# Two attentions on one core: projections of the self attention spread over twice as many blocks, and the weighted sum cut in two by queries

## The reference, cut to what matters

```python
qkv = x @ w_qkv.T                                  # self attention
scores = einsum('bhqd,bhkd->bhqk', q, k) * scale + bias
out = einsum('bhqk,bhkd->bhqd', softmax(scores), v)
x = layernorm(x + out @ w_proj.T + b_proj)         # called x1 in the kernel
scores = einsum('bqhd,bkhd->bhqk', x, ctx) * scale2
x = layernorm(x + einsum('bhqk,bkhd->bqhd', softmax(scores), ctx))   # x2
x = layernorm(x + experts(x))                      # not touched by the change
```

## Time and profile before

| what | value |
|---|---|
| three timed runs | 1044.22, 1048.89 and 1048.36 us; median 1048.36 us |
| profiled execution | span 1045.2 us from the first to the last instruction; no other time of its own is given |
| busy in that span | PE 934.1 us (89%), ACT 747.5 us (72%), DVE 703.3 us (67%), POOL 297.5 us (28%) |
| the 16 bodies | from 37.3 us to about 716 us of the span; the expert stage follows |

### The profile page before, as it was taken

One profiled execution on the slowest core, in us unless ns is written; L12 is line 12 of the kernel. 1 busy time (PEld: TensorE's weight loads), 2 busy tenths in 40 slices (PEclk: granted clock), 3 DMA queues, 4 the chain that ended last, 5 costly groups with the idle time before them and its releaser, 6 DMA issues. The chain is left out here.

```text
span 1045.2 us, 17700 instructions
## 1 busy us (share of the span) xinstructions
PE 934.1 (89%) x5301; PEld 514.6 (49%) x5301; DVE 703.3 (67%) x1836; ACT 747.5 (72%) x1414; POOL 297.5 (28%) x337
## 2 busy tenths in 40 slices
PE   5599999999999999999999998996189999999991
PEld 2133444444444433333333333332179988988991
DVE  5277777677787788356556565585457887887883
ACT  1378777787878778899898895893047766766761
POOL 4043132231404111011222123123323534444443
PEclk9699999999999999999999997997589999999996
DMA  7989596978687675987876793751263533443450
GB/s 208 207 229 251 109 256 143 316 142 252 143 247 187 185 201 88 181 199 161 160 155 114 157 174 68 144 120 41 76 216 115 202 137 121 169 180 127 163 208 30
DMA packets 74844, 172.04 MB, mean 165 GB/s; under 512 B 16657, under 2 KB 36039, under 8 KB 64712
## 3 DMA queue, kind: packets, MB, share of 16 engines
q1 hardware_dynamic: 67944, 156.36, 60.4%
q0 software_dynamic: 6496, 14.16, 3.9%
q10 hardware_dynamic: 320, 0.52, 0.1%
HBM read 122.23 MB, written 53.73 MB: 168 GB/s over the span
## 5 line engine op out<-in xcount | busy, mean ns | idle before, releaser
L742 ACT ACTIVATE probs<-sc 128x512 f32<-128x512 f32 x1024 | 528.9, 608 | 117.7 <-DVE sc L829 80.4
L497 PE MATMUL sc<-qst,kst 57*128 57x512 f32 (+1 forms) x1024 | 268.4, 473 | 18.2 <-DMA qst<-s_qk 12.8
L829 DVE TENSOR_TENSOR sc<-sc,strip 128x308 f32<-128x308 f32 (+1 forms) x512 | 192.8, 430 | 101.2 <-PE sc L497 100.5
L509 PE MATMUL ot<-probs,vals 128*32 128x512 f32 x1600 | 214.0, 607 | 0.1
L497 PEld LDWEIGHTS sc<-qst,kst 57*128 57x128 f32 (+1 forms) x1024 | 118.6, 187 | 191.8 <-ACT probs L742 147.7
L1691 ACT ACTIVATE f_h<-f_h_ps,par 128x384 f32<-128x384 f32 x104 | 60.9, 586 | 31.0 <-PE f_h_ps L1601 31.0
L1768 DVE TENSOR_TENSOR f_h_lo<-f_h,f_h_hi 128x384 fp32r<-128x384 f32 x104 | 73.4, 706 | 13.7 <-DVE f_h_hi L1766 5.7
L1849 POOL DMA_INDIRECT home<-s_x,get_ids x45 | 53.6, 1190 | 72.5 <-issue 42.4
L1766 DVE CAST f_h_hi<-f_h 128x384 fp32r<-128x384 f32 x104 | 37.1, 356 | 39.7 <-ACT f_h L1691 39.5
L509 PE MATMUL ms<-probs,vals 128*32 128x512 f32 x448 | 61.9, 627 | 0.0
L1862 POOL DMA_INDIRECT out<-f_normed,f_put_ids x39 | 43.1, 1106 | 64.6 <-ACT f_normed L1725 56.1
(11 more groups left out here) (189 smaller groups left out, 1604.7 us busy)
## 6 DMA issues: line engine op xcount, KB each, us to landing
s_qk<-w_hi SPq DMA_DIRECT2D x32, 512.0 KB, 7.3
strip<-in_w_all SPq DMA_DIRECT2D x16, 1024.0 KB, 7.7
f_raw<-in_w_all SPq DMA_DIRECT2D x14, 1024.0 KB, 6.3
s_x<-x SPq DMA_DIRECT2D x8, 1026.0 KB, 11.0
kst<-s_qk SPq DMA_DIRECT2D x32, 256.0 KB, 6.1
qst<-s_qk SPq DMA_DIRECT2D x32, 256.0 KB, 7.2
s_x_parts<-split SPq DMA_DIRECT2D x16, 512.0 KB, 8.8
kst<-s_ctx_parts SPq DMA_DIRECT2D x32, 256.0 KB, 6.6
```

What stands on the lines that cost most here:

```text
L497: nc.tensor.matmul(sc[j][:], kst[at:at + rows, i, P * c:P * c + P], qst[at:at + rows, i, :], start=True, stop=True).then_inc(scored, 1)
L509: last = nc.tensor.matmul(sums_bank(n, g)[32 * j:32 * j + 32, :], vals[:, c, 4 * g + j, :], probs[:, k % KEPT, j, :], start=(c == 0), stop ...
L742: nc.scalar.activation(probs[:, k % KEPT, j, :], sc[j][:], ACT.Exp, scale=scale).then_inc(exped, 1)
L829: nc.vector.tensor_tensor(sc[j][:, lo:hi], sc[j][:, lo:hi], band_backwards(rank_of(4 * g + j), at, hi - lo), ALU.add).then_inc(biased, 1)
```

## The change

It does four things. `attend` takes the place of `scores` and `weigh_behind`: in each block of both attentions PE now makes two heads' scores, the weighted sum of 256 queries, the other two heads' scores, and the weighted sum of the other 256 queries. `project_qk` is cut in two by input channels (d = 0 and 1, three matmuls each): queries and keys of pair 0 are made in blocks 0 to 3, those of pair 1 in blocks 12 to 15. The output projection and the values begin one block earlier. The tiles of PSUM are assigned anew, so that one transpose of x1 moves from block 15 to block 1 of the next body, and its store a body later. The x of batch b+2 gets a buffer of its own (`later_xT`, in the space of `x2`), is loaded before the store of x1, and POOL splits it in two halves.

```diff
-            def scores(n, k):
+            def scores(n, k, two):
...
-                for j in range(4):
+                for j in range(2 * two, 2 * two + 2):
...
-                pe.wait_ge(exped, UNITS * n + 4 * k + 4)
+                if half == 0:
+                    pe.wait_ge(exped, UNITS * n + 4 * k + 4)
                 for j in range(4):
-                    last = nc.tensor.matmul(sums_bank(n, g)[32 * j:32 * j + 32, :], vals[:, c, 4 * g + j, :],
-                                            probs[:, k % KEPT, j, :], start=(c == 0), stop=(c == NC - 1))
-                last.then_inc(summed, 1)
...
+                    last = nc.tensor.matmul(sums_bank(n, g)[32 * j:32 * j + 32, some], vals[:, c, 4 * g + j, :],
+                                            probs[:, k % KEPT, j, some],
+                                            start=(c == 0 and half == 0), stop=(c == NC - 1 and half == 1))
+                if half == 1:
+                    last.then_inc(summed, 1)
...
+            def attend(n, k):
+
+                for half in range(2):
+                    scores(n, k, half)
+                    weigh_behind(n, k, half)
...
-            def project_qk(b, i):
...
+            def project_qk(b, i, d):
...
+                terms = [term for term in terms_of(b) if term[2] == d]
...
-                if 5 <= k < 9:
-                    project_out(b, k - 5)
-                if k in (14, 15):
-                    turn_x1(b, 15 - k)
+                if k == 1 and b > 0:
+                    turn_x1(b - 1, 0)
+                if 4 <= k < 8:
+                    project_out(b, k - 4)
+                if k == 14:
+                    turn_x1(b, 1)
+                if k == 15 and b == B - 1:
+                    turn_x1(b, 0)
...
                 if k < 4:
-                    project_qk(b, k)
-                if 9 <= k < 13:
-                    project_v(b, (k - 9) // 2, (k - 9) % 2)
+                    project_qk(b, k // 2, k % 2)
+                if 8 <= k < 12:
+                    project_v(b, (k - 8) // 2, k % 2)
+                if k >= 12:
+                    project_qk(b, 2 + k % 2, k // 14)
```

SP's program of a self body, with the pair 1 transfers now inside the body that needs them:

```diff
                     sp.dma_start(xnat[:], io["x"][b].rearrange("(c p) n -> p c n", p=P)).then_inc(ld_xnat, 16)
+                if b > 1:
+                    store_x1_parts(b - 2, 1)
+                if b > 0:
+                    store_parts(b, 2)
+                    store_parts(b, 3)
+                if b > 1:
+                    store_x1_parts(b - 2, 0)
+                if b > 0:
+                    load_pair(b, 1)
...
-                if b < B - 1:
-                    store_parts(b + 1, 2)
-                    store_parts(b + 1, 3)
...
+                if b < B - 2:
+                    wait(sp, x_lo_ready, DC * b)
+                    sp.dma_start(later_xT, io["xT"][b + 2].rearrange("(c p) n -> p c n", p=P)).then_inc(ld_xT, 16)
                 if b > 0:
                     store_x1(b - 1)
...
-                load_pair(b + 1, 1)
-                if b > 0:
-                    store_x1_parts(b - 1)
+                if b == B - 1:
+                    load_pair(B, 1)
```

More of the change, by code:

```diff
@@ L281, in halt, with turned_x1 @@
             eng.drain()
+        def turned_x1(b, i):
+            return (ms[0] if b == B - 1 and i == 0 else ms[2])[:]
         def store_last(sp):
@@ L524, in terms_of @@
                 return [(w, x, d) for d in range(DC) for w, x in ((w_qkv_hi, x_hi), (w_qkv_hi, x_lo), (w_qkv_lo, x_hi))]
-            def project_qk(b, i):
[L528 to L537, removed]
+            def project_qk(b, i, d):
+                if d == 0:
+                    if i == 0:
+                        wait(pe, ld_xT, 16 * min(b, 1))
+                        if b == 2:
+                            pe.wait_ge(w_halved, 1)
+                        wait(pe, qk_lo, 4 * b - 1)
+                    elif i == 1:
+                        wait(pe, qk_lo, 4 * b)
+                    elif i == 2:
+                        pe.wait_ge(qk_lo, 4 * b + 1)
+                        wait(pe, out_read, 2 * (b - 1))
+                    else:
+                        pe.wait_ge(qk_lo, 4 * b + 2)
+                        wait(pe, v_nat, 2 * b + 1 if b > 0 else 0)
+                if i == 0 and b > 1:
+                    pe.wait_ge(x_lo_ready, DC * (b - 2) + d + 1)
@@ L538, in project_qk @@
                 col = C * (i % 2) + P * (i // 2)
-                terms = terms_of(b)
-                for n, (w, x, d) in enumerate(terms):
+                terms = [term for term in terms_of(b) if term[2] == d]
+                for n, (w, x, _) in enumerate(terms):
                     last = nc.tensor.matmul(ms[i % 2][:], w[:, d, col:col + P], x[:, d, :],
-                                            start=(n == 0), stop=(n == len(terms) - 1))
-                last.then_inc(qk_mm, 1)
+                                            start=(d == 0 and n == 0), stop=(d == DC - 1 and n == len(terms) - 1))
@@ L545, in project_v @@
+                if d == DC - 1:
+                    last.then_inc(qk_mm, 1)
+                elif b > 0 and i == 3:
+                    last.then_inc(first_half_used, 1)
             def project_v(b, i, t):
-                if t == 0:
-                    wait(pe, qk_lo, 4 * b + 4 - i)
+                if t == 0 and i == 0:
+                    pe.wait_ge(qk_lo, 4 * b + (4 if b == 0 else 2))
                 if t == 0 and i == 1:
-                    wait(pe, out_read, 2 * (b - 1))
+                    wait(pe, out_read, 2 * b - 3)
@@ L576, in turn_x1 @@
                 pe.wait_ge(have_x1, b + 1)
-                if i == 0:
-                    wait(pe, v_nat, min(2 * (b + 2) + 1, 2 * B))
+                if i == 1:
+                    wait(pe, v_nat, min(2 * (b + 2) + 2, 2 * B))
+                    pe.wait_ge(out_read, 2 * b + 1)
+                elif b < B - 1:
+                    pe.wait_ge(xt_lo, 2 * b + 1)
+                else:
+                    pe.wait_ge(out_read, 2 * B)
                 for t in range(NC):
-                    last = nc.tensor.transpose(ms[1 + i][:, P * t:P * t + P], x1[:, t, P * i:P * i + P], ident[:])
+                    last = nc.tensor.transpose(turned_x1(b, i)[:, P * t:P * t + P], x1[:, t, P * i:P * i + P], ident[:])
                 last.then_inc(xt_mm, 1)
@@ L707, in tensor_program @@
             for i in range(4):
-                project_qk(0, i)
+                for d in range(DC):
+                    project_qk(0, i, d)
             pe.wait_ge(ld_wv, 16)
@@ L719, in tensor_program @@
             for k in range(BLOCKS - BEHIND, BLOCKS):
-                weigh(2 * B - 1, k)
+                for half in range(2):
+                    weigh(2 * B - 1, k, half)
             pe.wait_ge(exped, 2 * UNITS * B)
@@ L1360, in self_body @@
                     split_weights()
-                if b < B - 2:
-                    split_x(b + 2)
                 for g in range(G - 1):
                     copy_v(b + 1, g)
+                if b < B - 2:
+                    for d in range(DC):
+                        split_x(b + 2, d)
             def cross_body(c):
```

99 lines of the change are left out of this document (54 added, 45 removed).

## The result

| | before | changed |
|---|---|---|
| timed runs | 1044.22, 1048.89, 1048.36, 1047.29 us | 1068.93, 1063.19, 1068.38, 1095.36 us |
| median | 1047.82 us | 1068.66 us |
| profiled execution, span | 1045.2 us | 1067.1 us |

The ratio is 1.0185 with an interval of 1.0135 to 1.0235: the change makes the kernel slower, by 1.4 to 2.4%. The forecast was 1047 us with a range of 1036 to 1062 us.

A forecast was written before the change was run, and what follows sets the result against it. The prediction expected PE to be full throughout, each body lasting the sum of PE's prices. Self bodies -6.2 us and cross bodies +4.6 gave -1.6: 1048.4 - 1.6 = 1047 us, range 1036 to 1062.

The forecast's parts named there:

- the one on the cross bodies: Cross attention: PE's prices make bodies 1 to 7 36.5 us against 35.9, six bodies × 0.6 = +3.6 us; together +4.6.
- body 5's stall: Cross body 5: its 44.9 us come from PE and DVE waiting elsewhere and stay, so no term.
- Prices on PE: Attention blocks: pair of scores 0.43 us, half a sum 0.56, half a projection 0.91; a self body 48.0 us.
- Bodies 1 and 3: Self attention: waits for x go; body 1 from 50.2 to 47.4 us (-2.8), body 3 from 50.1 to 48.0 (-2.1).
- Self body 7: Last self body, without projections to prepare: 40.0 us, between PE's bound of 37.7 and the present 42.8, so -2.8.
- Cross bodies 0 and 1: First two cross bodies: body 0 37.7 us against 36.7 (+1.0), body 1 36.5 against 35.9 (+0.6).
- The expert stage: The stage outside the two attentions: the prediction had no term for it.
- Cheaper edges: Attention blocks: hidden weight loads or shrinking edges save 25 or 29 us (1022 or 1018), half about 1034; chance 0.22.
- Pair 1 late: Self bodies: PE stands at block 8 until pair 1's loads land; 1.5 us late gives 1057 us; chance 0.22.
- PE full and unable to hide anything: Filled bodies: any wait for DVE or ACT adds directly; 0.1 us a block is 22 us, half gives 1058; chance 0.13.

The follow-up runs named there:

- the first kernel without the stall: The changed kernel with DVE's four weight split steps moved from cross body 5 to block 0 of cross bodies 3 to 6: 1047.04 us, ratio 0.998.
- the second: The changed kernel with DVE's four weight split steps moved from cross body 5 to block 7 of cross bodies 3 to 6: 1042.16 us, ratio 0.9948.

## Why the prediction was wrong, step by step

**The step that failed** is the one on the cross bodies: cross body 6 was priced like its neighbours ("Six bodies × 0.6 = +3.6 us"), and body 5's stall was said to "stay". It did stay, but the clock that falls with it was left out of the sum. The row of cross body 5 showed a clock of 0.87; the question not asked was how long the new order would run at that clock. Measured: +19.8 us in body 6 instead of +0.6, of which 18.8 are the clock's. The half order in two bodies of the kernel before brings this loss alone, and every order with two changes a block avoids it.

Outside cross body 6 the attentions cost +8.1 us where the sum has -2.2, and the expert stage gave back 5.9. So even the rest came near the forecast by two errors that partly cancel.

The other steps:

- **Prices on PE** (pair of scores, half sum, half projection): right. Plain self bodies came to 48.3 us (forecast 48.0), cross bodies to 36.7 (36.5). Over self bodies 0 to 6 the sum was -3.4 us and -1.3 was measured; it is these tenths, in every body.
- **Bodies 1 and 3** lost their waits for x as said: 47.9 and 48.4 us.
- **Self body 7**, -2.8 forecast, +1.2 measured. ACT and DVE were said to be "as close as PE"; in block 4 they were later than PE:

```profile
380.46 1.36 DVE L889 TENSOR_TENSOR normed<-turned,rden 128x256 f32<-128x256 f32 x1
```

```profile
383.40 0.99 PE L508 MATMUL sc<-qst,kst 57*128 57x512 f32 x2 [1.01 <-ACT probs L782]
...
386.51 2.07 PE L598 MATMUL ms<-w_out,onrm 128*128 128x256 f32 x4
388.52 0.66 PE L508 MATMUL sc<-qst,kst 57*128 57x512 f32 x2
```

  PE waits, the clock drops to 1.2 GHz for 3.4 us (385.49 to 388.90), and the output projection takes 2.01 us (386.51 to 388.52) instead of 1.06. That DVE's chain, now a block earlier, causes the wait was read from these rows and not tried.
- **Cross bodies 0 and 1**: +1.0 and +0.6 forecast, +2.0 and +1.7 measured. The sum on PE is right for the unloaded blocks; in body 1, for one, the first sum of a group waited for the values:

```profile
461.88 0.64 PE L522 MATMUL ot<-probs,vals 128*32 128x256 f32 x8 [0.83 <-POOL vals L1319]
```

- **The expert stage**, forecast at no change, became 5.9 us shorter. It gave back about a fifth of the loss, and hid it. One instruction of DVE goes with it. Before, with POOL's copy that starts inside it:

```profile
894.52 1.72 DVE L1768 TENSOR_TENSOR f_h_lo<-f_h,f_h_hi 128x384 fp32r<-128x384 f32 x1 [0.15 <-DVE f_h_hi L1766]
894.98 0.83 POOL L1859 COPY f_keep<-home 128x771 f32<-128x771 f32 x1
```

  and in the round that answers to it in the changed kernel:

```profile
920.97 0.56 DVE L1821 TENSOR_TENSOR f_h_lo<-f_h,f_h_hi 128x384 fp32r<-128x384 f32 x1 [0.15 <-DVE f_h_hi L1819]
921.43 0.84 POOL L1912 COPY f_keep<-home 128x771 f32<-128x771 f32 x1
```

  The trace of before has such a long one in every round of 20 us from 120 us into the stage on, that of the changed kernel in every second; 5 of them by 1.16 us make 5.8 us, an estimate that fits the 5.9. All 13 long ones of before, and all 7 of the changed kernel, have that copy of POOL starting 0.44 to 0.58 us behind their own start, and no instruction without it is long; but six of the changed kernel have the copy in the same place and are short, as at 920.97. All experiments made from the changed kernel have the shorter stage (322 to 326 us where it was 329.6), those made from the kernel before do not (330 and 331 us). So the copy goes with the delay; what decides between the two cases stays open, and nothing was tried on it.
- **Rivals.** Cheaper edges: no; half a sum costs 0.57 us and a pair of scores 0.43, so the edge stays whole at every change. The Trainium skill, "TensorEngine Tiling (Array Packing)", key properties, says that a change of tiling mode drains the engine; the 0.14 and 0.20 us for the extra edges agree. Pair 1 late: no; no self body has a gap at block 8, and its cover held (the kernel with whole sums everywhere, with shorter bodies, waited 0.55 us). PE full and unable to hide anything: the time falls on its side, but not by its mechanism, which was 0.1 us a block everywhere; plain self bodies have no such gaps.

## What to carry to other kernels

When a profile shows a dip of PE's clock behind a stall, price the change at both clocks, and ask how long the new code would run at the lower: here the stall cost 7 us with one order of the work and 26 with the other. Count changes of the matmul's shape rather than its pieces: back to back two halves cost no more than the whole, but two more changes cost 0.35 us a block. If a change has several parts, measure them apart: all but the interleaving was worth 17 us here (6 of them in the untouched expert stage), and stood hidden behind an order that lost 39 (1068.7 against 1029.6 us).

## What the runs showed of the hardware

TensorE can stay at 1.2 GHz for 58 us in which it has no gap (58.03 of 58.03 us busy in the kernel before with the half order in two bodies; the last 55.10 of 58.03 in the changed kernel), when it changes between 48-row score matmuls and 32-column sums four times a block. With two changes a block it was back after 10.2 to 17.1 us behind the stall in the same place (1.93 to 4.04 us), in five kernels (the one before, whole sums everywhere, and those with whole sums behind, whole sums between, and half sums behind the scores of the cross attention). Four changes a block do not always keep it there: after other falls it was back in 3.4 us (self body 7 of the changed kernel, cross body 6 of the first kernel without the stall, cross body 4 of the second). In both long cases it rose only around the transposes of x2 (blocks 10 and 11 of cross body 6), at 696.1 and 694.2 us, and the two short ones in the cross attention also ended behind such transposes. So the count of changes and the side work in the blocks that follow both go with the length of the low clock. Which of their properties sets it was not shown, and no run moved the side work alone.

DVE's `f_h_lo`, 0.56 us by itself, took 1.71 to 1.84 us in 20 of the 26 cases in which POOL's copy `f_keep` started inside its time (the kernel before and the changed one), and never without it.
